# Products of the values-keys matrix with the output weight: three fp16 passes of split halves in place of one fp32 matmul each

## The chip, the cores and the metric

The kernel runs on one core of a Trainium2 chip. The metric is device time in microseconds of one execution; smaller is better.

## The reference, cut to what matters

```python
xn = _layernorm(x)                                     # x is [1250, 1024]
x = x + gnn(xn, edge_index, W, b) + mix(xn[None], Wq, bq, ..., Wo, bo)[0]
x = x + ffn(_layernorm(x)[None], clip_x, clip_down, w_gate, w_up, w_down)[0]

def mix(x, ...):                                       # H = 16 heads of DH = 64
    q = relu(split_heads(x @ Wq + bq))
    k = relu(split_heads(x @ Wk + bk))
    v = split_heads(x @ Wv + bv)
    context = einsum('bhld,bhkd->bhlk', q, k) / (l * DH)
    attn = einsum('bhlk,bhkd->bhld', context, v)
    return attn @ Wo + bo                              # heads side by side
def gnn(x, edge_index, W, b):                          # self loops, symmetric norm
    h = x @ W
    return relu(segment_sum(h[src] * norm[:, None], dst) + b)
```

There is no softmax between q k and v, so attn @ Wo = q @ M, where M is, for each head, (k^T v) / (l DH) times that head's rows of Wo. The kernel forms M once: it is [1024, 1024].

## The kernel before, in words

Nodes lie in T = 10 tiles of 128 rows (1250, the last is short). Matmuls of x with a weight are done in fp16: both sides are scaled by 256 and split into a high half and a low half (value minus high), and three products (high high, high low, low high) are added in PSUM. One such product of a 128-row tile with a 512-column half of a weight is 8 x 3 = 24 matmuls (node_unit, L498 to L516, the matmul is L509).

The order of work, written out by hand on each engine: keys and values in two column halves (with the counting of edges beside them), q, the graph projections g, the matrix M, then tile by tile (tile_b) the aggregation over edges (L687), q @ M (L713) and the residual, then the feed-forward part.

What the change touches lies between g and tile_b:

- **g tiles.** h over two column halves, t over ten tiles. TensorE (g_tile, L612) writes tile t into proj[t % 2] and waits before it for S["h_lo"] of tile t - 2, whose bank it takes. ScalarE (L870 to L877) writes the high half h16 from PSUM, signal h_hi; VectorE (L1205 to L1213) the low half, signal h_lo. Both have a hardware loop over pairs of tiles, with the tile's address from a register. TensorE has a loop too, but tiles (0,0) and (0,1) stand ahead of it, with the degree sums (L623) between them.
- **kvs**, the keys-values products kv_acc (128x128 blocks for pairs of heads, the diagonal 64x64 blocks wanted). VectorE clears kvs (L1189, fp32, 128x1024) and copies four groups of diagonal blocks from PSUM with the scale (L1195). This stands in VectorE's queue behind the degrees and ahead of the first h_lo.
- **The products.** TensorE multiplies kvs (8 pairs of heads) with wo, 2 column halves of the output weight: 16 fp32 matmuls of 512 columns (L646), into four banks in turn (tp[0], tp[1], proj[0], proj[1]). Product 2 takes proj[0] and waits for all 20 h_lo. Product i >= 4 waits for m_lo of i - 4. ScalarE copies the high half into m16 (L883, signal m_hi), VectorE the low half (L1220, signal m_lo); after product 1's, VectorE also makes the counts of tile 0 in fp16 (a_tile, L1202).
- **SyncE** loads wo[0] once the degrees are summed and the column maxima are there (L336 to L338), wo[1] after g tile (0,9) (L339), into places that earlier weights have left. After product 7 come the gnn bias and x tiles 0 and 1 (L341 to L344), after product 15 the bias bo (L346) and the first feed-forward weights; these take the place of wo and of kvs.
- **After it.** VectorE's evacuation in tile_b (L1281, L1284) needs x with bo added by POOL (L457), which waits for bo (L453); TensorE's next aggregation into the same banks waits for VectorE.

The lines that a sentence can't say:

```python
m_bank = tp + proj
wo = [part(RAW, K, HALF), part(0, K, HALF)]
kvs = part(XT + T * D, PAIRS, P)                       # fp32
if i >= 4:                                             # L642, TensorE, product i
    pe.wait_ge(SM["m_lo"], i - 3)
elif i == 2:
    pe.wait_ge(S["h_lo"], 2 * T)
pe.matmul(m_bank[i % 4][:, :], kvs[:, p, :], wo[n][:, p, :], start=True,
          stop=True).then_inc(SM["prod_full"], 1)
step(dve.memset(kvs, 0.0))                             # L1189, VectorE
```

Of the kernel before, what the change touches and what calls it, by code (L numbers as in the profile page):

```python
# [53 lines left out]
def gps_layer(nc, x, src, dst, gnn_W, gnn_b, Wq, bq, Wk, bk, Wv, bv, Wo, bo,  # L54
              clip_x, clip_down, w_gate, w_up, w_down, out):
    with ExitStack() as ctx:
# [3 lines left out]
        def sems(*names):  # L60
            return {n: ctx.enter_context(nc.semaphore(n)) for n in names}
# [10 lines left out]
        def part(at, *dims, dt=F32):  # L72
            size = 1
            for d in dims:
                size *= d
            words = size * {F16: 2, BF16: 2, I8: 1}.get(dt, 4) // 4
            a = mem[:, at:at + words]
            if dt != F32:
                a = a.bitcast(dt)
            if len(dims) == 2:  # L80
                a = a.rearrange("p (a b) -> p a b", b=dims[1])
            if len(dims) == 3:
                a = a.rearrange("p (a b c) -> p a b c", b=dims[1], c=dims[2])
            return a
# [17 lines left out]
        xT = part(XT, 2 * K, NP, dt=F16)  # L102
        kvs = part(XT + T * D, PAIRS, P)
        assert XT + T * D + D == 8 * SLOT + 11 * D
# [3 lines left out]

        wo = [part(RAW, K, HALF), part(0, K, HALF)]
        m16 = [part(XT + i * SLOT, K, D, dt=F16) for i in range(2)]  # L110

# [56 lines left out]
        def col(n=1):  # L168
# [21 lines left out]
        SE = sems("e_hot", "e_mm")  # L190
        SM = sems("wo_in0", "wo_in1", "gb_in", "bo_in", "kvs", "sources", "deg_full", "deg_ready", "dinv", "prod_full",
                  "m_hi", "m_lo", "max_col", "max_T")
# [84 lines left out]
        def _(sp):  # L277
# [64 lines left out]
            sp.dma_start(gb_b, gnn_b.rearrange("(a n) -> a n", a=1).broadcast_to([P, D])).then_inc(SM["gb_in"], 16)  # L342
            sp.dma_start(x_t[0], x[0:P, :]).then_inc(SB["xb_in0"], 16)
            sp.dma_start(x_t[1], x[P:2 * P, :]).then_inc(SB["xb_in1"], 16)  # L344
            sp.wait_ge(SM["prod_full"], 2 * PAIRS)
# [127 lines left out]
        def _(pe):  # L473
# [164 lines left out]
            for n in range(2):  # L638
                pe.wait_ge(SM[f"wo_in{n}"], 16)
                for p in range(PAIRS):  # L640
                    i = PAIRS * n + p
                    if i >= 4:  # L642
                        pe.wait_ge(SM["m_lo"], i - 3)
                    elif i == 2:
                        pe.wait_ge(S["h_lo"], 2 * T)
                    pe.matmul(m_bank[i % 4][:, :], kvs[:, p, :], wo[n][:, p, :], start=True,  # L646
                              stop=True).then_inc(SM["prod_full"], 1)

# [127 lines left out]
        def _(act):  # L776
# [91 lines left out]


            for h in range(2):  # L870
                with act.Fori(0, T // 2) as t2:
                    for par in range(2):
                        t = 2 * t2 + par
                        act.wait_ge(S["g_full"], T * h + t + 1)
                        act.wait_ge(SM["dinv"], 3)
                        act.activation(h16[:, bass.ds(t, 1), h * HALF:(h + 1) * HALF].rearrange("p a n -> p (a n)"),  # L876
                                       proj[par][:, :], ACT.Copy, scale=dinv_up[:, bass.ds(t, 1)]).then_inc(S["h_hi"], 1)  # L877


            for i in range(2 * PAIRS):  # L880
                n, p = i // PAIRS, i % PAIRS
                act.wait_ge(SM["prod_full"], i + 1)
                act.activation(m16[0][:, p, n * HALF:(n + 1) * HALF], m_bank[i % 4][:, :], ACT.Copy).then_inc(SM["m_hi"], 1)  # L883

# [73 lines left out]
        def _(dve):  # L958
# [232 lines left out]
            for b in range(2):  # L1191
                acc = kv_acc[b][:, :].rearrange("p (q n) -> p q n", n=P)
                for h in range(2):
                    r = slice(h * DH, (h + 1) * DH)
                    dve.tensor_scalar(kvs[r, 4 * b:4 * b + 4, r], acc[r, :, r], M_UP / (N * DH), None,  # L1195
                                      ALU.mult).then_inc(SM["kvs"], 1)

# [5 lines left out]


            for h in range(2):  # L1205
                with dve.Fori(0, T // 2) as t2:
                    for par in range(2):
                        t = 2 * t2 + par
                        dve.wait_ge(S["h_hi"], T * h + t + 1)
                        high, low = [h16[:, bass.ds(t, 1), a * D + h * HALF:a * D + (h + 1) * HALF].rearrange("p a n -> p (a n)")  # L1210
                                     for a in range(2)]
                        dve.scalar_tensor_tensor(low, proj[par][:, :], dinv_up[:, bass.ds(t, 1)], high, ALU.mult,  # L1212
                                                 ALU.subtract).then_inc(S["h_lo"], 1)  # L1213


            for i in range(2 * PAIRS):
                n, p = i // PAIRS, i % PAIRS
                dve.wait_ge(SM["m_hi"], i + 1)
                s = slice(n * HALF, (n + 1) * HALF)
                dve.tensor_tensor(m16[1][:, p, s], m_bank[i % 4][:, :], m16[0][:, p, s], ALU.subtract).then_inc(SM["m_lo"], 1)  # L1220
                if i == 1:
                    a_tile(0, 0)
# [188 lines left out]
```

## Time and profile before

| | |
|---|---|
| median of 3 runs | 761.18 us (760.9 to 761.96) |
| the profiled execution's own time | 761.22 us |
| its span, first to last instruction | 759.4 us |
| mean granted TensorE clock over the span | 0.981 of full |
| TensorE matmuls busy | 720.4 us, 95% |
| VectorE, ScalarE, GpSimd (POOL) busy | 490.1, 216.3, 272.1 us |
| L509 matmuls (all uses of node_unit) | 1440, 327.6 us busy, mean 381 ns |
| L646 as traced | 32 records for the 16 products |

How to read it: times are microseconds from the start of the span, unless marked ns. PE is TensorE's matmuls, PEld its weight loads, which run beside them; DVE is VectorE, ACT ScalarE, POOL GpSimd, SP SyncE. Matmuls are pipelined: a record (380 ns for 512 columns) is longer than the time from one start to the next, so the pace is read from a stretch with its count. A trailing bracket is idle time of the engine ahead of the row, and what ended it. ACTq and DVEq are the sequencers of these engines, with register work and waits. The chain of waits is followed back from the last instruction: at each step to what released it, or to the instruction before it on its engine.

### The profile page before, as it was taken

The page shows a single profiled execution, that of the slowest core. Times are in us where ns is not written, and L with a number is a line of the kernel's source. Part 1 is how long each engine was busy: PE and PEld are TensorE (multiplying, and loading weights), DVE is VectorE, ACT ScalarE, POOL GpSimd, SP SyncE. Part 2 cuts the span into 40 slices and gives each one's busy share as a digit, 9 for nine tenths or more (in the row PEclk, how much of TensorE's full clock was granted, in tenths as well). Part 3 has the DMA queues.
Part 4 walks back from the last instruction along what each step waited for, and adds up shares of the span by engine and source line. Part 5 has one row for each costly group of instructions (what it writes and reads, how often), then busy time and mean ns, then how long its engine had stood idle before and what let it go on. Part 6 is the DMA issues. An engine that isn't in the chain of part 4 may idle for free.

```text
span 759.4 us, 12399 instructions
## 1 busy us (share of the span) xinstructions
PE 720.4 (95%) x3889; PEld 370.9 (49%) x3892; DVE 490.1 (65%) x968; ACT 216.3 (28%) x363; POOL 272.1 (36%) x403
## 2 busy tenths in 40 slices
PE   4999999999999999999999999999999999994984
PEld 2455555555555544666544444444444444443551
DVE  7878887887666565557711111677777797757467
ACT  5133235542333244454111111401101110013450
POOL 5567677997666565530100000111111101110018
PEclk9999999999999999999999999999999999997997
DMA  9743322640000000003200300501111120000006
GB/s 344 215 123 71 91 55 73 197 164 13 0 0 0 0 2 1 2 1 111 84 28 0 110 0 0 163 26 56 57 49 48 48 66 30 22 0 1 1 13 258
DMA packets 35166, 47.87 MB, mean 63 GB/s; under 512 B 18883, under 2 KB 19915, under 8 KB 35121
## 3 DMA queue, kind: packets, MB, share of 16 engines
q1 hardware_dynamic: 35120, 47.28, 19.6%
q8 instruction: 27, 0.44, 0.2%
q14 instruction: 19, 0.15, 0.1%
HBM read 37.96 MB, written 5.12 MB: 57 GB/s over the span
## 4 chain that ended last, share of the span: by engine, by line
PE 73%; issue 13%; DVE 6%; POOL 4%; ACT 1%; DMA 1%; DVEq 1%; POOLq 0%; SPq 0%; ACTq 0%
PE bank L509 31%; PE bank L582 14%; PE bank L713 12%; PE bank L687 10%; POOL mem L468 2%; PE bank L494 2%; PE bank L646 2%; DVE mem L1001 2%; PE bank L526 2%; DVE counts L1091 1%; ACT mem L796 1%; DMA mem<-in_x 1%; DVE mem L1017 1%; POOL cols L396 1%; DVE hot_dst L1078 0%
## 5 line engine op out<-in xcount | busy, mean ns | idle before, releaser
L509 PE MATMUL bank<-mem 128*128 128x512 f16 x1440 | 327.6, 381 | 3.3 <-ACT mem L796 2.0
L509 PEld LDWEIGHTS bank<-mem 128*128 (+1 forms) x1440 | 137.9, 98 | 156.5 <-issue 5.1
L420 POOL TENSOR_SCALAR hot_src<-iota_p,src_col 125x128 bf16<-125x128 bf16 x252 | 174.5, 707 | 14.1 <-issue 14.1
L1091 DVE TENSOR_TENSOR counts<-bank,counts 128x120 f32 x328 | 92.4, 282 | 49.2 <-issue 8.4
L582 PE MATMUL bank<-mem 128*128 128x384 f16 (+1 forms) x576 | 107.5, 344 | 0.0
L713 PE MATMUL bank<-mem 128*128 128x512 f16 x480 | 105.4, 379 | 0.0
L687 PE MATMUL bank<-mem 128*128 128x512 f16 x400 | 88.0, 379 | 0.0
L582 PEld LDWEIGHTS bank<-mem 128*128 128x128 f16 (+1 forms) x576 | 55.3, 98 | 43.6
L713 PEld LDWEIGHTS bank<-mem 128*128 128x128 f16 x480 | 46.7, 98 | 54.3
L1212 DVE SCALAR_TENSOR_TENSOR mem<-bank,cols,mem 128x512 f32 x20 | 15.0, 751 | 81.8 <-ACT mem L876 81.8
L816 ACT ACTIVATE src_gap<-iota_p,loT 125x128 bf16<-125x128 bf16 x84 | 33.6, 399 | 115.2 <-PE bank L494 106.6
L459 POOL TENSOR_TENSOR cols<-cols 128x1 f32<-128x1 f32 x10 | 5.6, 555 | 166.5 <-DVE cols L1301 166.5
L457 POOL TENSOR_TENSOR mem<-mem 128x1024 f32<-128x1024 f32 x10 | 23.5, 2346 | 114.5 <-DMA mem<-in_L_mix_bo 114.5
L687 PEld LDWEIGHTS bank<-mem 128*128 128x128 f16 x400 | 39.1, 98 | 47.3 <-issue 0.6
L1078 DVE TENSOR_TENSOR hot_dst<-iota_w,keyT 125x480 bf16<-125x480 bf16 x84 | 55.1, 658 | 0.0
L417 POOL COPY src_col<-loT 125x3 f32 (+1 forms) x84 | 25.7, 306 | 69.6 <-PE bank L494 64.8
L1001 DVE SCALAR_TENSOR_TENSOR mem<-mem 128x2048 f16<-128x2048 f32 x16 | 36.8, 2303 | 6.7 <-ACT mem L796 6.7
L876 ACT ACTIVATE mem<-bank,cols 128x512 f32 x20 | 13.7, 687 | 91.9 <-PE bank L509 82.5
L1291 DVE SCALAR_TENSOR_TENSOR mem<-bank,mem 128x512 f32<-128x512 f32 x20 | 13.8, 692 | 40.0 <-PE bank L713 39.9
L468 POOL TENSOR_TENSOR mem<-mem 128x720 f32<-128x720 f32 (+1 forms) x10 | 18.7, 1897 | 50.6 <-DVE mem L1385 50.6
L494 PEld LDWEIGHTS bank<-hot_dst,hot_src 125*128 125x128 bf16 x328 | 24.5, 97 | 20.7 <-DVE counts L1091 1.9
L796 ACT ACTIVATE mem<-mem 128x2048 f16<-128x2048 f32 x16 | 30.4, 1904 | 14.7 <-DMA mem<-in_L_mix_Wk 6.0
(153 smaller groups left out, 681.8 us busy)
## 6 DMA issues: line engine op xcount, KB each, us to landing
mem<-in_x SPq DMA_DIRECT2D x18, 512.0 KB, 3.6
out_x<-mem SPq DMA_DIRECT2D x9, 512.0 KB
mem<-in_L_mix_Wk SPq DMA_DIRECT2D x4, 1024.0 KB, 9.4
mem<-in_L_mix_Wv SPq DMA_DIRECT2D x4, 1024.0 KB, 8.4
mem<-in_L_mix_Wq SPq DMA_DIRECT2D x4, 1024.0 KB, 5.2
mem<-in_L_gnn_W SPq DMA_DIRECT2D x4, 1024.0 KB, 5.2
mem<-in_L_mix_Wo SPq DMA_DIRECT2D x2, 2048.0 KB, 7.9
mem<-in_L_ffn_w_down SPq DMA_DIRECT2D x4, 352.0 KB, 3.0
```

The costliest lines, as they stand in the source:

```text
L420: pool.tensor_scalar(hot_src[0:EC, i, c, :], iota_p[0:EC, :], src_col[0:EC, i, c:c + 1], None, ALU.is_equal).then_inc(S["hot_src_ready"], 1)
L468: pool.tensor_tensor(x2[:, t, s], x2[:, t, s], y_t[t % 4][:, s], ALU.add).then_inc(SC["y_ready1"], 1)
L494: last = pe.matmul(agg[i][:, c * WC:(c + 1) * WC], hot_src[0:EC, i, c, :], hot_dst[0:EC, i, c, :], start=(c == 0), stop=True, skip_group_c ...
L509: last = pe.matmul(o[:, :], xT[:, a * K + k, bass.ds(t * P, P)], w16[i][:, k, b, :], start=(at == 0), stop=(at == len(parts) - 1))
L582: last = pe.matmul(proj[j % 2][:, 0:n * P], w_q.rearrange("p a n -> p (a n)"), xT[:, a * K + k, t0 * P:(t0 + n) * P], start=(k == 0 and a ...
L687: last = pe.matmul(agg[n][:, :], a_t[par][:, s, :], h16[:, s, b * D + n * HALF:b * D + (n + 1) * HALF], start=(fresh and s == 0 and b == 0 ...
L713: last = pe.matmul(proj[n][:, :], q_k, m16[b][:, k, n * HALF:(n + 1) * HALF], start=(k == 0 and a == b), stop=(k == K - 1 and a == 1))
L796: act.activation(w16[i][:, 4 * c:4 * c + 4, 0, :], w_raw[i][:, 4 * c:4 * c + 4, :], ACT.Copy, scale=W_UP).then_inc(S["w_hi"], 1)
L816: act.activation(src_gap[0:EC, i, :], iota_p[0:EC, :], ACT.Abs, bias=loT[0:EC, bass.ds(g * G + G - 1, 1)], scale=-1.0).then_inc(S["src_gap ...
L1001: dve.scalar_tensor_tensor(w16[i][:, s, 1, :], w_raw[i][:, s, :], W_UP, w16[i][:, s, 0, :], ALU.mult, ALU.subtract).then_inc(S["w_lo"], 1)
L1078: dve.tensor_tensor(hot_dst[0:EC, i], iota_w[0:EC], key, ALU.is_equal).then_inc(S["hot_dst_ready"], 1)
L1091: dve.tensor_tensor(window, agg[i][:, k * WC:(k + 1) * WC], window, ALU.add).then_inc(S["adj_added"], 1)
```

## The change

The products run as three fp16 matmuls of 512 columns each. For this, kvs becomes fp16 with a high and a low half (the same bytes), and the output weight is split into halves, 256 times as large, beside the g tiles: ScalarE's and VectorE's loops over the g tiles are written out, and after tiles (0,4), (0,7), (1,4) and (1,6) each takes a quarter of the weight (128x2048). The halves lie partly where earlier quarters of wo were. The evacuations of the products scale by 1/256; VectorE's turns from a subtraction into a multiply-subtract. SyncE's load of x tile 1 waits for four more products, since its place now holds halves of the weight.

```diff
--- before.py
+++ after.py
@@ -100,13 +100,15 @@
         bq_rows = part(QT + 6 * D, P)[0:K]
         XT = QT + T * D
         xT = part(XT, 2 * K, NP, dt=F16)
-        kvs = part(XT + T * D, PAIRS, P)
+        kvs = part(XT + T * D, 2 * PAIRS, P, dt=F16)
         assert XT + T * D + D == 8 * SLOT + 11 * D
         sources = part(RAW, NP)
         w16_q = part(2 * SLOT, 4 * K, HALF, dt=F16)
         h16 = part(2 * SLOT, T, 2 * D, dt=F16)
 
         wo = [part(RAW, K, HALF), part(0, K, HALF)]
+        wo16 = [[part(at, K, HALF, dt=F16) for at in ats] for ats in ((EXTRA, RAW), (RAW + 2 * D, 0))]
+        WO_AFTER = {(0, 4): (0, 0), (0, 7): (0, 1), (1, 4): (1, 0), (1, 6): (1, 1)}
         m16 = [part(XT + i * SLOT, K, D, dt=F16) for i in range(2)]
 
         x2 = part(QT - D, T, D)
@@ -188,7 +190,7 @@
                  "k_relu", "kv_done", "q_full", "x_hi", "x_lo", "xT_in0", "xT_in1", "src_gap", "hot_src_act", "counts_diag", "q_relu", "q_hi", "q_lo", "g_full", "h_hi", "h_lo", "hot_dst_ready",
                  "hot_src_ready", "adj_mm", "adj_added", "counts_set")
         SE = sems("e_hot", "e_mm")
-        SM = sems("wo_in0", "wo_in1", "gb_in", "bo_in", "kvs", "sources", "deg_full", "deg_ready", "dinv", "prod_full",
+        SM = sems("wo_in0", "wo_in1", "gb_in", "bo_in", "kvs", "kvs_hi", "wo_hi", "wo_lo", "sources", "deg_full", "deg_ready", "dinv", "prod_full",
                   "m_hi", "m_lo", "max_col", "max_T")
         SB = sems("xb_in0", "xb_in1", "x_bias", "a_ready", "mix_full", "agg_full", "mix_moved", "agg_moved",
                   "b_var", "b_rstd", "b_max", "a_more", "a_more_used")
@@ -341,6 +343,7 @@
             sp.wait_ge(SM["prod_full"], PAIRS)
             sp.dma_start(gb_b, gnn_b.rearrange("(a n) -> a n", a=1).broadcast_to([P, D])).then_inc(SM["gb_in"], 16)
             sp.dma_start(x_t[0], x[0:P, :]).then_inc(SB["xb_in0"], 16)
+            sp.wait_ge(SM["prod_full"], PAIRS + 4)
             sp.dma_start(x_t[1], x[P:2 * P, :]).then_inc(SB["xb_in1"], 16)
             sp.wait_ge(SM["prod_full"], 2 * PAIRS)
             sp.dma_start(bo_b, bo.rearrange("(a n) -> a n", a=1).broadcast_to([P, D])).then_inc(SM["bo_in"], 16)
@@ -636,15 +639,19 @@
 
             pe.wait_ge(SM["kvs"], 4)
             for n in range(2):
-                pe.wait_ge(SM[f"wo_in{n}"], 16)
                 for p in range(PAIRS):
                     i = PAIRS * n + p
+                    if p in (0, 4):
+                        pe.wait_ge(SM["wo_hi"], 2 * n + p // 4 + 1)
+                        pe.wait_ge(SM["wo_lo"], 2 * n + p // 4 + 1)
                     if i >= 4:
                         pe.wait_ge(SM["m_lo"], i - 3)
                     elif i == 2:
                         pe.wait_ge(S["h_lo"], 2 * T)
-                    pe.matmul(m_bank[i % 4][:, :], kvs[:, p, :], wo[n][:, p, :], start=True,
-                              stop=True).then_inc(SM["prod_full"], 1)
+                    for a, b in ((0, 0), (0, 1), (1, 0)):
+                        last = pe.matmul(m_bank[i % 4][:, :], kvs[:, a * PAIRS + p, :], wo16[n][p // 4][:, 2 * (p % 4) + b, :],
+                                         start=(a == b), stop=(a == 1))
+                    last.then_inc(SM["prod_full"], 1)
 
 
             def piece(i):
@@ -867,20 +874,27 @@
             act.activation(clip[:, 2:4], clip[:, 0:2], ACT.Exp, scale=-1.0).then_inc(SC["exp"], 1)
 
 
+            def wo_high(n, c):
+                act.wait_ge(SM[f"wo_in{n}"], 16)
+                act.wait_ge(SM["wo_lo"], 2 * n + c)
+                act.activation(wo16[n][c].rearrange("p (k b) n -> p k b n", b=2)[:, :, 0, :], wo[n][:, 4 * c:4 * c + 4, :], ACT.Copy,
+                               scale=W_UP).then_inc(SM["wo_hi"], 1)
+
             for h in range(2):
-                with act.Fori(0, T // 2) as t2:
-                    for par in range(2):
-                        t = 2 * t2 + par
-                        act.wait_ge(S["g_full"], T * h + t + 1)
-                        act.wait_ge(SM["dinv"], 3)
-                        act.activation(h16[:, bass.ds(t, 1), h * HALF:(h + 1) * HALF].rearrange("p a n -> p (a n)"),
-                                       proj[par][:, :], ACT.Copy, scale=dinv_up[:, bass.ds(t, 1)]).then_inc(S["h_hi"], 1)
+                for t in range(T):
+                    act.wait_ge(S["g_full"], T * h + t + 1)
+                    act.wait_ge(SM["dinv"], 3)
+                    act.activation(h16[:, t, h * HALF:(h + 1) * HALF], proj[t % 2][:, :], ACT.Copy,
+                                   scale=dinv_up[:, t:t + 1]).then_inc(S["h_hi"], 1)
+                    if (h, t) in WO_AFTER:
+                        wo_high(*WO_AFTER[h, t])
 
 
             for i in range(2 * PAIRS):
                 n, p = i // PAIRS, i % PAIRS
                 act.wait_ge(SM["prod_full"], i + 1)
-                act.activation(m16[0][:, p, n * HALF:(n + 1) * HALF], m_bank[i % 4][:, :], ACT.Copy).then_inc(SM["m_hi"], 1)
+                act.activation(m16[0][:, p, n * HALF:(n + 1) * HALF], m_bank[i % 4][:, :], ACT.Copy,
+                               scale=1.0 / W_UP).then_inc(SM["m_hi"], 1)
 
 
             act.wait_ge(SC["c_step"], 1)
@@ -1193,7 +1207,14 @@
                 for h in range(2):
                     r = slice(h * DH, (h + 1) * DH)
                     dve.tensor_scalar(kvs[r, 4 * b:4 * b + 4, r], acc[r, :, r], M_UP / (N * DH), None,
-                                      ALU.mult).then_inc(SM["kvs"], 1)
+                                      ALU.mult).then_inc(SM["kvs_hi"], 1)
+            for b in range(2):
+                acc = kv_acc[b][:, :].rearrange("p (q n) -> p q n", n=P)
+                for h in range(2):
+                    r = slice(h * DH, (h + 1) * DH)
+                    dve.wait_ge(SM["kvs_hi"], 2 * b + h + 1)
+                    dve.scalar_tensor_tensor(kvs[r, PAIRS + 4 * b:PAIRS + 4 * b + 4, r], acc[r, :, r], M_UP / (N * DH),
+                                             kvs[r, 4 * b:4 * b + 4, r], ALU.mult, ALU.subtract).then_inc(SM["kvs"], 1)
 
             def counts_tile(t):
                 return counts[:, bass.ds(t * P * T, P * T)].rearrange("p (n s) -> p s n", s=T)
@@ -1202,22 +1223,28 @@
                 dve.tensor_scalar(a_t[par], counts_tile(t), float(COUNT_MAX), None, ALU.min).then_inc(SB["a_ready"], 1)
 
 
+            def wo_low(n, c):
+                dve.wait_ge(SM["wo_hi"], 2 * n + c + 1)
+                high, low = [wo16[n][c].rearrange("p (k b) n -> p k b n", b=2)[:, :, a, :] for a in range(2)]
+                dve.scalar_tensor_tensor(low, wo[n][:, 4 * c:4 * c + 4, :], W_UP, high, ALU.mult,
+                                         ALU.subtract).then_inc(SM["wo_lo"], 1)
+
             for h in range(2):
-                with dve.Fori(0, T // 2) as t2:
-                    for par in range(2):
-                        t = 2 * t2 + par
-                        dve.wait_ge(S["h_hi"], T * h + t + 1)
-                        high, low = [h16[:, bass.ds(t, 1), a * D + h * HALF:a * D + (h + 1) * HALF].rearrange("p a n -> p (a n)")
-                                     for a in range(2)]
-                        dve.scalar_tensor_tensor(low, proj[par][:, :], dinv_up[:, bass.ds(t, 1)], high, ALU.mult,
-                                                 ALU.subtract).then_inc(S["h_lo"], 1)
+                for t in range(T):
+                    dve.wait_ge(S["h_hi"], T * h + t + 1)
+                    high, low = [h16[:, t, a * D + h * HALF:a * D + (h + 1) * HALF] for a in range(2)]
+                    dve.scalar_tensor_tensor(low, proj[t % 2][:, :], dinv_up[:, t:t + 1], high, ALU.mult,
+                                             ALU.subtract).then_inc(S["h_lo"], 1)
+                    if (h, t) in WO_AFTER:
+                        wo_low(*WO_AFTER[h, t])
 
 
             for i in range(2 * PAIRS):
                 n, p = i // PAIRS, i % PAIRS
                 dve.wait_ge(SM["m_hi"], i + 1)
                 s = slice(n * HALF, (n + 1) * HALF)
-                dve.tensor_tensor(m16[1][:, p, s], m_bank[i % 4][:, :], m16[0][:, p, s], ALU.subtract).then_inc(SM["m_lo"], 1)
+                dve.scalar_tensor_tensor(m16[1][:, p, s], m_bank[i % 4][:, :], 1.0 / W_UP, m16[0][:, p, s], ALU.mult,
+                                         ALU.subtract).then_inc(SM["m_lo"], 1)
                 if i == 1:
                     a_tile(0, 0)
             dve.wait_ge(SM["prod_full"], 2 * PAIRS)
```

## Rows read from the trace of the kernel before

**Rows 1.** The page, busy time of the engines.

```profile
PE 720.4 (95%) x3889; PEld 370.9 (49%) x3892; DVE 490.1 (65%) x968; ACT 216.3 (28%) x363; POOL 272.1 (36%) x403
```

**Rows 2.** Chain of waits, 360 to 510: start us, us, what (count).

```profile
374.04 98.47 PE bank L509 x456
...
472.73 0.70 ACT mem L876
...
473.72 0.76 DVE mem L1212
...
474.52 12.28 PE bank L646 x28
486.81 8.63 PE bank L687 x40
...
505.80 4.32 PE bank L687 x20
```

**Rows 3.** Timeline of the products: start us, us, engine, line, operation, shapes, count.

```profile
472.34 1.88 PE L646 MATMUL bank<-mem 128*128 128x512 f32 x4
...
474.38 1.28 DVE L1220 TENSOR_TENSOR mem<-bank,mem 128x512 f16<-128x512 f32 x2
...
475.58 1.31 DVE L1202 TENSOR_SCALAR mem<-counts 128x1280 f16<-128x1280 uint16 x1
...
476.80 1.92 DVE L1220 TENSOR_TENSOR mem<-bank,mem 128x512 f16<-128x512 f32 x3
...
478.26 0.60 ACT L883 ACTIVATE mem<-bank 128x512 f16<-128x512 f32 x1 [0.26 <-PE bank L646]
...
478.89 0.69 DVE L1220 TENSOR_TENSOR mem<-bank,mem 128x512 f16<-128x512 f32 x1 [0.17 <-ACT mem L883]
...
479.75 0.69 DVE L1220 TENSOR_TENSOR mem<-bank,mem 128x512 f16<-128x512 f32 x1 [0.17 <-ACT mem L883]
```

**Rows 4.** Groups by form: busy us, mean ns | idle us before, releaser.

```profile
L1001 DVE SCALAR_TENSOR_TENSOR mem<-mem 128x2048 f16<-128x2048 f32 x16 | 36.8, 2303 | 6.7 <-ACT mem L796 6.7
...
L1284 DVE SCALAR_TENSOR_TENSOR mem<-bank,mem 128x512 f32<-128x512 f32 x20 | 13.8, 692 | 1.5
...
L1023 DVE MEMSET cols<- 128x256 f32 x1 | 0.3, 272 | 0.1
...
L796 ACT ACTIVATE mem<-mem 128x2048 f16<-128x2048 f32 x16 | 30.4, 1904 | 14.7 <-DMA mem<-in_L_mix_Wk 6.0 <-DMA mem<-in_L_mix_Wv 3.6 <-DMA mem<-in_L_mix_Wq 2.8
```

**Rows 5.** Timeline 371 to 381, columns as in rows 3.

```profile
374.91 0.91 DVE L1189 MEMSET mem<- 128x1024 f32 x1 [0.28 <-DVE clip L1187]
375.86 1.78 DVE L1195 TENSOR_SCALAR mem<-bank 64x256 f32<-64x256 f32 x4
...
377.19 0.69 ACT L876 ACTIVATE mem<-bank,cols 128x512 f32 x1 [9.37 <-POOL cols L451]
378.18 0.75 DVE L1212 SCALAR_TENSOR_TENSOR mem<-bank,cols,mem 128x512 f32 x1 [0.54 <-ACT mem L876]
379.08 1.84 PEld L509 LDWEIGHTS bank<-mem 128*128 x10 [0.36 <-issue]
```

**Rows 6.** The page, DMA issues: count, KB each, us to landing.

```profile
mem<-in_L_mix_Wo SPq DMA_DIRECT2D x2, 2048.0 KB, 7.9
```

**Rows 7.** Timeline after the products, columns as in rows 3.

```profile
491.40 2.35 POOL L457 TENSOR_TENSOR mem<-mem 128x1024 f32<-128x1024 f32 x1 [114.52 <-DMA mem<-in_L_mix_bo]
```

**Rows 8.** Timeline of TensorE alone, two idle times elsewhere, columns as in rows 3.

```profile
32.06 5.35 PE L509 MATMUL bank<-mem 128*128 128x512 f16 x24 [1.24 <-DVE mem L1017]
...
702.52 0.62 PE L736 MATMUL bank<-ident,mem 128*128 128x128 bf16 x8 [2.17 <-DVE mem L1341]
```

**Rows 9.** Windows: busy PE, PEld, DVE, ACT, POOL, then granted clock, DMA share, GB/s.

```profile
32.00:34.00 2.00, 1.94 (x9) 0.90 (x10) 1.48 (x3) 1.01 (x2) 0.00 (x0) 1.00 0.08 17
...
704.00:706.00 2.00, 1.85 (x9) 1.67 (x9) 0.11 (x1) 1.78 (x3) 0.00 (x0) 0.50 0.00 0
706.00:708.00 2.00, 1.93 (x7) 0.84 (x7) 1.93 (x4) 0.00 (x0) 0.00 (x0) 0.71 0.00 0
```

## The prediction

> **What bounds the kernel now.** I read the page first: TensorE is busy 95% of the span [rows 1], so only what TensorE issues, or what makes it wait, can move the end. The chain of waits around the changed place says where. It runs through TensorE alone for 456 matmuls of the graph projections (L509, tiles (0,1) to (1,9), 98.47 us), which is 0.2159 us per fp16 matmul of 512 columns; leaves it for one evacuation on ScalarE and one on VectorE; then takes 12.29 us of L646 (from 474.52 to 486.81) and enters the aggregation L687 [rows 2]. Everything from L687 on is one serial stretch of TensorE, so a microsecond gained or lost before 486.81 reaches the end, unless a later load is missed.
>
> The timeline of the products shows their neighbours. VectorE's low halves (L1220) start 0.86 us apart, 0.03 us after ScalarE's 0.60 us: they follow TensorE's fp32 pace of 0.86 us per product. When VectorE is behind it goes faster: three take 1.92 us, so with 0.69 us for each record the starts are 0.61 apart. After the first two stands the count conversion L1202, with 1.22 us from its start to the next L1220 [rows 3].
>
> **The products.** An fp32 product costs 0.86 us; three fp16 passes cost 3 x 0.2159 = 0.648. Their weight loads run beside them, as L509's do. For the 14 products behind the wait for the last h_lo this is 14 x 0.86 = 12.04 against 9.07: **-2.97 us**. (12.29 - 12.04 = 0.25 is the first weight load and the last drain; it stays.) The first two products gain nothing: they end at 472.34 + 1.30 = 473.64 and the third must still wait for h_lo.
>
> That wait gets shorter, since both evacuation loops are written out. Now ScalarE starts 0.22 us after TensorE's end (472.51 to 472.73) and VectorE 0.29 after ScalarE's end [rows 2]; the written-out L1220 starts 0.03 after its releaser [rows 3]. I take 0.03 for VectorE and 0.05 for ScalarE: **-0.42 us**, product 2 at 474.10 instead of 474.52. Bounds: 0 and -0.5. At the other 18 tile ends the shorter lags gain nothing, TensorE being a tile ahead.
>
> What is late next is VectorE. h_lo starts at 473.29, m_lo 0 follows 0.66 later as now (473.72 to 474.38), m_lo 1 at 474.55, the conversion at 475.15, m_lo 2 at 476.37 and ends at 477.06. Product 6 uses its bank again and could start at 474.20 + 4 x 0.648 = 476.79, but starts 0.14 (signal and weight load) after 477.06: **+0.41 us**. After that VectorE's 0.61 and ScalarE's 0.60 stay under 0.648, and TensorE sets the pace. L1220 becomes a multiply-subtract from PSUM; L1284, the same kind on 128x512, has 0.692 us [rows 4], as L1220 has. The pace of 0.61 is bounded above by 0.69 (a rival, below). ScalarE's constant scale costs nothing here.
>
> Products together: -2.97 - 0.42 + 0.41 = **-2.98 us**.
>
> **The key-value matrix.** It is made ahead of h_lo 0, and this isn't hidden. Now the memset starts at 374.91 and takes 0.91, L1195 starts at 375.86 and its four take 1.78 (to 377.64); VectorE then waits 0.54 for ScalarE, and h_lo 0 ends at 378.93. TensorE's weight load of tile (0,2), which wants bank 0 back, comes at 379.08 after 0.36 of idle [rows 5]. So h_lo 0 has no slack: each further VectorE microsecond stands on the path.
>
> Added are four multiply-subtracts of 64x256 from PSUM, the form of the tensor_scalars with one more input. Four of those are 1.78, or 0.45 from start to start; I take 4 x 0.45 = 1.81. None of the four overlapped the one before it, so it is no less than 4 x 0.42 = 1.7; from above 4 x 0.69 = 2.8, L1284's full-size record [rows 4], which is far off, having twice the columns. The own-engine wait on kvs_hi is four instructions old and met, save for the pipeline.
>
> The memset keeps its bytes but goes from 1024 fp32 to 2048 fp16 elements. No row has a 2-byte memset. By bytes it stays at 0.91. By elements: 256 take 0.272 [rows 4] and 1024 take 0.912, 0.833 ns each, so 2048 take 1.77, 0.85 more. Below, fewer than 0.91 would need packing that no row shows. I take 1.77, since size in elements is all that the rows show it to follow. The Trainium skill (VectorE: DVE Perf Modes, "Zero memsets can be issued as uint32 (trn2)") says a memset takes one cycle per element whatever the type, which speaks for the slow end; with its 0.96 GHz that would be 2.13 us for 2048, 1.2 more than now, but the same sum gives 1.07 for 1024 where the trace has 0.91, so its rate is not taken; the total by it would be 0.4 us higher.
>
> h_lo 0 then starts at 377.64 + 0.85 + 1.81 + 0.03 = 380.33 instead of 378.18: **+2.15 us**, all of it TensorE idle ahead of tile (0,2). ScalarE (h_hi 1) isn't behind it, and h_lo 1 is wanted only 5.2 us later.
>
> **The halves of the output weight.** Four splits of 128x2048: 1.90 us on ScalarE and 2.30 on VectorE each, by L796 and L1001, the same shapes [rows 4]. Behind h_hi and h_lo of a tile they end 0.05 + 0.70 + 1.90 + 2.30 + 0.1 = 5.1 us after its end, about when the next tile's ends (24 x 0.2159 = 5.18); h_lo there is due one tile after that. Cost nothing; if the load of Wo were missing they would block ScalarE, but it is issued at about 374, takes 7.9 us to land [rows 6], and the first split comes after tile (0,4), near 395; the second load is issued after tile (0,9) near 421 and used after tile (1,4).
>
> **Loads on SyncE.** x_t[1] now waits for product 12, and bo_b stands behind it. bo_b lands at 491.40 now, 4.6 us after L687's start; POOL adds 2.35 to 493.75, and VectorE's four evacuations (about 3 us) free the banks by 497, wanted at 505.80 [rows 2, 7]. Sharing the engines with x_t[1], of the same size, it is late by 4.6 at most: 8.8 us of slack. Weight pieces move along with product 16. Nothing.
>
> **Sum:** -2.98 + 2.15 = -0.83. The profiled execution took 761.22 (span 759.4), 0.04 over the median of 761.18: **760.4 us**. A measurement of this kernel can tell about 0.2%, 1.5 us, from no change, and the forecast lies inside that.
>
> **Rivals.** (1) The memset goes by bytes: the stall is 1.30, the net -1.68, 759.5 us. For it: the region is the same. Against: the element slope.
>
> (2) **The clock falls**: the new idle of TensorE at 379 is some 2.1 us. After an idle of 1.24 us at 32.06 the granted clock was 1.00; after one of 2.17 us at 702.52 it was 0.50 in 704 to 706 and 0.71 in 706 to 708 [rows 8, 9], the lower level, 1.2 GHz. [...] Against it: before 702 TensorE did short products with pauses, before 379 it streams 512 columns without one. Price: 2 x 0.50 + 2 x 0.29 = 1.58 us of streaming, net +0.75: slower than before, 762.0 us.
>
> (3) VectorE paces the products: each m_lo takes its full 0.69. m_lo 11 ends at 476.37 + 10 x 0.69 = 483.27, and L687 starts 0.38 later: net -0.45, 760.8 us. The Trainium skill (VectorE: DVE Perf Modes, "The DRAIN you can't avoid") has the next operation wait until the pipe is empty, which gives this case. The three in 1.92 us speak against it.
>
> **How the numbers follow.** Forecast 0.43, (1) 0.22, (2) 0.20, (3) 0.11, others 0.04. The range runs from (1) with the lags at their best, 759.1, to (2) with the multiply-subtracts 0.5 dearer, 762.5. Faster by over 0.2% needs -1.52: about half of (1), the tail of the forecast and part of the others, 0.26. Slower by over 0.2% needs (2) and more on top, 0.08. Same 0.66.
>
> **What would show it.** In the timeline: memset near 1.77; four multiply-subtracts near 0.42; h_lo 0 ending near 381.1; an idle of 2.1 at tile (0,2), granted clock 1.00 behind it. h_lo 19 starting 0.8 after TensorE's end, not 1.2. Products 0.65 apart from product 7 on, one short stall before product 6. The stretch from the end of L509 to L687 14.3 - 3.0 = 11.3 us. L713 and the tiles after as before. I am wrong if h_lo 0 has slack, if the clock is below 1 behind 381, or if products wait for m_lo throughout.

## The result, and the profile after

| | before | changed |
|---|---|---|
| median | 761.57 us (760.9 to 762.85, 6 runs) | 759.25 us (758.75 to 759.92, 6 runs) |
| ratio | | 0.9968, 95% interval 0.9955 to 0.9981 |
| profiled execution, own time (span) | 761.22 (759.4) | 759.92 (758.1) |

The change makes the kernel 0.3% faster, 2.4 us by the ratio (1.4 to 3.4 by its interval). The forecast was 760.4 in a range of 759.1 to 762.5, with "same within 0.2%" as the likeliest outcome (0.66); the ratio lies outside those 0.2%, the end of its interval touches them. The time is near that of rival (1), 759.5, but rival (1) saves 1.68 us and 2.4 were measured.

In the page of the changed kernel TensorE is as full as before:

```profile
PE 719.2 (95%) x3908; PEld 370.0 (49%) x3908; DVE 500.2 (66%) x976; ACT 223.7 (30%) x367; POOL 272.1 (36%) x403
```

The chain of waits from 360 to 520, which answers to [rows 2] (start us, us, what, count):

```profile
366.36 5.18 PE bank L512 x24
...
373.80 100.12 PE bank L512 x456
473.92 0.02 issue
473.94 0.70 ACT mem L887
474.64 0.02 issue
474.66 0.75 DVE mem L1236
475.41 1.20 DVE mem L1246 x2
476.61 1.25 DVE mem L1223
477.86 0.61 DVE mem L1246
...
478.51 6.65 PE bank L652 x30
485.16 8.63 PE bank L694 x40
```

Read it in two pieces. From the end of the g tiles to L694 (the aggregation, L687 before) it takes 485.16 - 473.92 = 11.24 us, where before it took 486.81 - 472.51 = 14.30: -3.06. Inside it the chain leaves TensorE for VectorE's two low halves, the conversion L1223 and the third low half, as the prediction's step had it. But the 456 matmuls of the g tiles take 100.12 us, against 98.47 in [rows 2]: 1.65 more. That wasn't expected. The timeline from 371 to 392 answers to [rows 5]:

```profile
374.67 0.91 DVE L1203 MEMSET mem<- 128x1024 uint32 x1 [0.28 <-DVE clip L1201]
...
375.61 1.78 DVE L1209 TENSOR_SCALAR mem<-bank 64x256 f16<-64x256 f32 x4
...
377.42 1.78 DVE L1216 SCALAR_TENSOR_TENSOR mem<-bank,mem 64x256 f16<-64x256 f32 x4
...
379.24 0.75 DVE L1236 SCALAR_TENSOR_TENSOR mem<-bank,cols,mem 128x512 f16<-128x512 f32 x1
380.70 0.69 ACT L887 ACTIVATE mem<-bank,cols 128x512 f16<-128x512 f32 x1 [3.28 <-PE bank L512]
```

The memset is one of 1024 uint32 elements and takes 0.91 us, not 1.77. The four multiply-subtracts take 1.78, as forecast. h_lo 0 ends at 379.99, 1.3 us later than 378.93 when both are counted from the degrees (373.70 here, 373.95 before). And yet TensorE shows no idle: tile (0,1) itself ends only near 380.6 (ScalarE's h_hi 1, which follows it, starts at 380.70). The windows of 2 us say why (busy PE, PEld, DVE, ACT, POOL, then the granted clock):

```profile
374.00:376.00 2.00, 2.00 (x9) 0.75 (x7) 1.65 (x5) 0.00 (x0) 1.95 (x1) 0.67 0.49 112
376.00:378.00 2.00, 2.00 (x6) 0.76 (x5) 1.84 (x6) 0.69 (x1) 0.51 (x2) 0.50 1.03 382
378.00:380.00 2.00, 2.00 (x10) 0.88 (x9) 1.90 (x4) 0.00 (x0) 0.00 (x0) 0.97 1.05 410
```

The granted clock is at its lower level (0.50, 1.2 GHz) for most of tile (0,1), right behind the degree sums. Tile (0,1) becomes longer than VectorE's delay and covers it. Before, all windows from 372 to 380 had 1.00 in the profiled execution; the middle one:

```profile
376.00:378.00 2.00, 2.00 (x11) 0.90 (x10) 1.55 (x4) 0.69 (x1) 0.70 (x3) 1.00 1.00 376
```

One pair of profiles, then, can't price the four multiply-subtracts, and it had to be asked whether the fall of the clock belongs to the change.

### The profile page after: what moved, and what is told of

The parts are those of the page before. It is cut to its first block, busy times and chain, and to the rows that moved or that the text cites. A ratio compares the mean times of both kernels' runs of the same rounds, so it can differ in the third digit from the quotient of the medians.

```text
span 758.1 us, 12288 instructions
## 1 busy us (share of the span) xinstructions
PE 719.2 (95%) x3908; PEld 370.0 (49%) x3908; DVE 500.2 (66%) x976; ACT 223.7 (30%) x367; POOL 272.1 (36%) x403
## 4 chain that ended last, share of the span: by engine, by line
PE 73%; issue 13%; DVE 7%; POOL 4%; ACT 1%; DMA 1%; DVEq 1%; POOLq 0%; SPq 0%
PE bank L512 31%; PE bank L585 14%; PE bank L720 12%; PE bank L694 10%; POOL mem L471 2%; PE bank L497 2%; DVE mem L1015 2%; PE bank L529 2%; DVE counts L1105 1%; ACT mem L803 1%; PE bank L652 1%; DMA mem<-in_x 1%; DVE mem L1031 1%; POOL cols L399 1%; DVE hot_dst L1092 0%
## 5 line engine op out<-in xcount | busy, mean ns | idle before, releaser
L694 PE MATMUL bank<-mem 128*128 128x512 f16 x400 | 88.0, 379 | 0.0
L694 PEld LDWEIGHTS bank<-mem 128*128 128x128 f16 x400 | 39.1, 98 | 47.0
L1236 DVE SCALAR_TENSOR_TENSOR mem<-bank,cols,mem 128x512 f16<-128x512 f32 x20 | 15.0, 751 | 67.8 <-ACT mem L887 67.8
L887 ACT ACTIVATE mem<-bank,cols 128x512 f16<-128x512 f32 x20 | 13.8, 688 | 86.1 <-PE bank L512 76.9
L826 ACT ACTIVATE hot_src<-src_gap,cols 125x128 bf16<-125x128 bf16 x84 | 33.7, 402 | 2.7
```

Source lines behind the costliest of these rows:

```text
L694: last = pe.matmul(agg[n][:, :], a_t[par][:, s, :], h16[:, s, b * D + n * HALF:b * D + (n + 1) * HALF], start=(fresh and s == 0 and b == 0 ...
L826: act.activation(hot_src[0:EC, i, G - 1, :], src_gap[0:EC, i, :], ACT.Relu, bias=ones[0:EC], scale=-1.0).then_inc(S["hot_src_act"], 1)
```

## The experiments

Two theories. **A**: the products save about 3.05 us; the work ahead of h_lo 0 costs about 1.3 us of TensorE idle, except in executions in which the clock falls in tile (0,1). **B**: the work ahead of h_lo 0 never stands on the path. To keep them from the noise of the rest of the kernel (the g tiles start anywhere from 366.36 to 367.42 in these profiles), I take from each profile the stretch from the start of g tile (0,0) to the start of the aggregation, both read in the chain of waits. In the kernel before, the stretch begins with this line (its end, 486.81, is in [rows 2]):

```profile
366.61 5.18 PE bank L509 x24
```

The fourth column is the same question for an earlier place, 14 to 18 us, long before anything that the change touches.

| kernel | stretch, us | clock fell at 374 to 378 | at 14 to 18 | median, us (runs) | ratio to before, 95% interval |
|---|---|---|---|---|---|
| before | 486.81 - 366.61 = 120.20 | no | yes | 761.57 (6) | |
| changed | 485.16 - 366.36 = 118.80 | yes | no | 759.25 (6) | 0.9968 [0.9955, 0.9981] |
| after_again | 485.67 - 366.86 = 118.81 | yes | no | 759.21 (8) | 0.9966 [0.9951, 0.998] |
| kvs_later | 485.95 - 367.16 = 118.79 | yes | no | 759.22 (10) | 0.9967 [0.9954, 0.9979] |
| loops_out | 486.59 - 366.88 = 119.71 | no | yes | 761.13 (12) | 0.9993 [0.9981, 1.0005] |
| four_more | 488.73 - 366.88 = 121.85 | yes | no | 762.57 (12) | 1.0008 [0.9997, 1.0019] |
| degrees_before | 486.44 - 366.85 = 119.59 | no | no | 760.62 (12) | 0.9986 [0.9975, 0.9996] |
| degrees_after | 484.24 - 366.37 = 117.87 | no | no | 757.75 (5) | 0.9954 [0.994, 0.9967] |
| degrees_kvs_later | 483.95 - 367.42 = 116.53 | no | no | 757.59 (5) | 0.9952 [0.9939, 0.9966] |
| memset_elements | 488.14 - 366.75 = 121.39 | no (later) | yes | 760.42 (10) | 0.9987 [0.9977, 0.9998] |
| waits_only | 485.10 - 366.63 = 118.47 | no | yes | 759.0 (1) | |
| a_tile_later | 485.27 - 366.84 = 118.43 | yes | no | 759.58 (1) | |
| products_both | 484.26 - 366.61 = 117.65 | no | yes | 758.29 (1) | |
| all_four | 482.40 - 366.72 = 115.68 | no | no | 756.9 (6) | 0.9938 [0.9923, 0.9953] |

The three kernels with one execution each serve for their stretch alone. Outside the stretch the fourteen profiled executions took between 639.9 and 641.9 us, so whole times differ by up to 2 us for reasons that lie elsewhere.

The two columns on the clock belong together. Of the ten profiles with all the degree sums in a row, the five that fell at 14 to 18 us did not fall at 374 to 378, and the five that did not fall there all fell at 374 to 378; each group holds kernels with the old and with the new products. The fall at 14 to 18 is in this line of the kernel before (0.56; the changed kernel has 1.00 there):

```profile
14.00:16.00 2.00, 1.89 (x6) 0.59 (x5) 2.00 (x3) 1.77 (x1) 2.00 (x3) 0.56 1.06 393
```

So whether the clock falls in tile (0,1) differs from execution to execution and goes with something that is there long before the changed place. Why the two exclude each other no run shows.

### The changed kernel again

No edit.

> The changed kernel once more, beside the parts below. Theory A (the chain of TensorE: the products save 3.06 us, the four multiply-subtracts ahead of h_lo 0 cost 1.3 us of TensorE idle, unless the granted clock falls behind the degree sums and makes tile (0,1) about 1.7 us longer, which hides them): times in two clusters, 1.7 to 1.8 us under the clean executions of before without that fall, 3.06 under those with it. Theory B (the multiply-subtracts never stand on the path): 3 us under before in both. Median 759.3 in A, 758.2 in B.

Median 759.21 (758.56 to 760.48), beside 29 runs of before with a median of 761.19 (760.39 to 763.79). The stretch is 118.81, the clock fell again. The lowest runs are 1.83 apart (758.56 and 760.39), the highest 3.31. That leans to A, but no more: the lowest and highest of 8 runs are set beside those of 29, and no pair of clusters is to be seen. Both kernels spread evenly, the rest of the kernel adding its own differences.

### kvs later

```diff
-            step(dve.memset(kvs, 0.0))
-            ...
+            def make_kvs():
+                step(dve.memset(kvs, 0.0))
+                ...
             for h in range(2):
                 for t in range(T):
                     ...
+                    if (h, t) == (0, 1):
+                        make_kvs()
```

> The whole making of kvs is moved behind h_lo of tile (0,1), so nothing but the degrees stands ahead of h_lo 0. Theory A: 1.3 us less than the changed kernel where the clock does not fall in tile (0,1), the same where it does; the idle at tile (0,2) is gone. 3.0 us under before in every execution. Theory B: as the changed kernel.

The profile fell on an execution with the lower clock. Its chain of waits has the same g tiles:

```profile
374.59 100.12 PE bank L512 x456
```

The same 100.12 us with h_lo 0 ending at 379.09, more than 2 us before TensorE was through with tile (0,1) (h_hi 1, which follows it, ends just ahead of h_lo 1's start at 382.22): the extra 1.65 us is the clock alone, and nothing of VectorE's lateness stands behind it. The lowest run, 758.0, is 0.56 under after_again's and the medians are equal. The expected "3.0 under before in every execution" is not seen in the medians (2.0), so this run by itself leaves A and B open.

### The loops written out alone

```diff
-                with act.Fori(0, T // 2) as t2:
-                    for par in range(2):
+                for t in range(T):
...
-                with dve.Fori(0, T // 2) as t2:
-                    for par in range(2):
+                for t in range(T):
```

> The kernel before with ScalarE's and VectorE's loops over the g tiles written out, nothing else. My step says -0.42 us, between the end of L509 and the third product: ScalarE starts 0.05 after TensorE's end and VectorE 0.03 after ScalarE's. Rival: the register work was not on the path, 0.

The chain of waits doesn't leave TensorE any more:

```profile
374.32 98.42 PE bank L509 x456
472.74 13.85 PE bank L646 x32
```

13.85 us instead of 14.30: -0.45, where I had -0.42. In the time it can't be told (0.9993, the interval holds 1).

### Four more operations in the kernel before

```diff
+            for b in range(2):
+                ...
+                    dve.wait_ge(SM["kvs"], 2 * b + h + 1)
+                    dve.scalar_tensor_tensor(kvs[r, 4 * b:4 * b + 4, r], acc[r, :, r], M_UP / (N * DH),
+                                             kvs[r, 4 * b:4 * b + 4, r], ALU.mult, ALU.max).then_inc(SM["kvs"], 1)
...
-            pe.wait_ge(SM["kvs"], 4)
+            pe.wait_ge(SM["kvs"], 8)
```

> The kernel before with four more operations of 64x256 from PSUM ahead of h_lo 0 (a scaled copy again, kept as the maximum with itself: same values). h_lo 0 ends 1.8 - 0 us later than before's 378.93. Theory A: +1.7 us where the clock does not fall in tile (0,1), the idle standing ahead of tile (0,2); 0 to 0.3 where it falls. Theory B: 0 always.

```profile
374.32 100.12 PE bank L509 x456
```

The clock fell in this profile, so the fall is no property of the new products. The stretch is 121.85 = 120.20 + 1.65: with the fall, four operations ahead of h_lo 0 cost nothing. That they cost without it this run doesn't show, as its one profile has the fall. The times lean that way (the median of 12 runs is 1.38 above before's, the lowest 1.29 above the lowest of 29), but the ratio of 1.0008 makes it 0.6 us, with an interval that holds no change.

### The degree sums inside tile (0,0)

The 20 one-column matmuls (10 sums, two passes each) stand between g tiles (0,0) and (0,1) for 2.1 us. Seven sums can be taken earlier:

```diff
+                    if at % 3 == 2 and at // 3 < len(degrees):
+                        degree(degrees[at // 3])
...
-            g_tile(0, 0, 0)
-            pe.wait_ge(SM["sources"], 1)
-            for n in range(T):
+            g_tile(0, 0, 0, degrees=range(7))
+            for n in range(7, T):
```

For this VectorE signals each quarter of the counts as it is done (src_part, not shown), and each sum waits for its own quarter.

> The changed kernel, with seven of the ten degree sums issued between the matmuls of g tile (0,0) and only three behind it. The stretch of one-column matmuls, after which the granted clock fell to 0.5 in three of four profiles, shrinks from 2.1 to about 0.7 us, and its weight loads run beside the 512-column matmuls. Theory A: no fall at 374 to 378, one cluster of times instead of two; the stretch itself saves 1.4 us; h_lo 0 has no cover, so TensorE idles 1.3 us at tile (0,2). About 757.4 us. If the fall has another cause it stays in most executions, tile (0,1) takes 1.7 us more and the times lie in two clusters again.

> The same, with kvs made behind h_lo of tile (0,1). Theory A: 1.3 us under degrees_after in every execution, about 756.1, and no idle at tile (0,2). Theory B (the multiply-subtracts never on the path): equal to degrees_after.

> The kernel before with seven degree sums inside g tile (0,0). No fall of the clock at 374 to 378, about 1.5 us under before, 759.6, in one cluster. The difference to degrees_after is then what the change is worth without the clock's part: -3.06 + 1.2 = -1.9 us.

In degrees_after the cost stands bare. The timeline:

```profile
378.65 1.41 DVE L1239 SCALAR_TENSOR_TENSOR mem<-bank,cols,mem 128x512 f16<-128x512 f32 x2
...
379.56 8.80 PE L512 MATMUL bank<-mem 128*128 128x512 f16 x40 [1.18 <-DVE mem L1239]
```

h_lo 0 ends at 379.41, TensorE starts 0.15 later, after 1.18 us of idle. (In the chain the stall is a little longer than that idle: from the start of g tile (0,0) to the end of the g tiles before has 472.51 - 366.61 = 105.90, and waits_only, which has the same idle of 1.18, 473.85 - 366.63 = 107.22, so 1.32 more.) The chain of waits now runs through the memset, the four copies, the four multiply-subtracts and h_lo 0. With kvs made later it does not. The g tiles in its chain:

```profile
374.25 98.44 PE bank L512 x456
...
483.95 8.63 PE bank L699 x40
```

against, in degrees_after,

```profile
379.56 93.43 PE bank L512 x432
...
484.24 8.63 PE bank L699 x40
```

The stretch is 116.53 against 117.87: 1.34 us for the order of VectorE's work alone. **Within the stretch this shows A's mechanism.** The time does not show it: 756.1 was expected and 757.59 measured, beside 757.75 for degrees_after, five runs each. What hides it is at least in part the clock elsewhere. The five runs of degrees_after have a mean granted clock of 0.9838 over the span, those of degrees_kvs_later 0.9818, and in the 61 runs of before beside these experiments the 19 at 0.983 or more have a median of 760.9, the 42 below it 761.95. In the profile of degrees_kvs_later, for one, TensorE idles 2.40 us at 31.82 and has a clock of 0.50 behind it, which none of the others has. That the 1.34 us reach the end is thus argued, not shown.

And the change itself, without the fall on either side: 119.59 to 117.87, -1.72 us. (The runs say more, 760.62 to 757.75; by the ratios 0.9986 and 0.9954 it is 2.4 us, with about 1 us of uncertainty on each. They don't contradict 1.72 and don't confirm it.) The same comes from before and waits_only (below), whose products last as long as the changed kernel's: 120.20 to 118.47, -1.73. With the fall on both sides, taking four_more for what before would be there (the one profile of before has no such fall): 121.85 to 118.80, -3.05.

The saving of the move I had too large: 1.4 to 1.5 us expected, 120.20 - 119.59 = 0.61 found. A sum between 512-column matmuls still takes 0.12 us of TensorE in the chain, against 0.21 in the row of twenty. By the ratio the runs gained 1.1 us; the 0.5 beyond the stretch would fit a fall that no longer comes in part of the executions. The profiles speak for that: of those without a fall at 14 to 18, five of five fell at 374 to 378 with the sums in a row, and none of the four with seven of them moved. (The move also shifts all behind it by 0.6 us, and no run separates the two.) The times still spread as widely as before (759.33 to 762.22), and "one cluster" was wrong.

### The memset by elements

```diff
-            step(dve.memset(kvs, 0.0))
+            step(dve.memset(kvs[:, :, 0:1], 0.0))
+            step(dve.memset(kvs[:, :, 1:P], 0.0))
```

> The changed kernel with kvs cleared in two pieces (column 0 of each block, then the other 127), which can't be read as 4-byte words. My step said 0.833 ns per element whatever its size: the memset of 2032 fp16 elements takes 1.76 us instead of 0.91, h_lo 0 ends 0.95 later (with the 0.1 of the small piece). If it goes by bytes: 0.91. Time: up to 0.9 over the changed kernel where the clock does not fall, about 0.3 to 0.9 where it does.

```profile
375.46 1.75 DVE L1204 MEMSET mem<- 128x2032 f16 x1 [0.49 <-DVE mem L1203]
...
381.79 6.39 PE L512 MATMUL bank<-mem 128*128 128x512 f16 x21 [2.42 <-DVE mem L1237]
```

The element rate holds: 1.75 us for 2032 two-byte elements, 0.833 ns each by the slope from [rows 4]. TensorE idles 2.42 us, 1.24 more than the 1.18, where 0.95 was expected: 0.84 is the memset, and the small piece ahead of it costs 0.40 and not 0.1, since the second memset starts 0.49 behind its end. And behind that idle comes what rival (2) described. The windows:

```profile
382.00:384.00 2.00, 2.00 (x8) 0.78 (x7) 0.28 (x1) 0.00 (x0) 0.00 (x0) 0.75 0.00 0
384.00:386.00 2.00, 2.00 (x6) 0.73 (x5) 0.00 (x0) 0.00 (x0) 0.00 (x0) 0.50 0.00 0
386.00:388.00 2.00, 2.00 (x9) 0.83 (x8) 0.00 (x0) 0.00 (x0) 0.00 (x0) 0.90 0.03 8
```

The chain has, for tiles (0,2) to (1,9) of this kernel and then of waits_only:

```profile
381.79 95.11 PE bank L512 x432
```

```profile
380.43 93.42 PE bank L512 x432
```

The fall costs 1.69 us; I had priced it 1.58. The stretch adds up: 118.47 + 1.24 + 1.69 = 121.40, found 121.39. The ratio has it 1.3 to 1.5 us above the changed kernel, more than the 0.9 expected.

### Product 2's wait, and the conversion

```diff
-                    elif i == 2:
-                        pe.wait_ge(S["h_lo"], 2 * T)
+                    elif i >= 2:
+                        pe.wait_ge(S["h_lo"], 2 * T - 3 + i)
```

```diff
-                if i == 1:
+                if i == 11:
                     a_tile(0, 0)
```

waits_only has the first, a_tile_later the second, products_both both.

> The changed kernel, product 2 waiting for 19 of the 20 h_lo (its bank was tile (1,8)'s), product 3 for all. Product 2 starts 0.4 us earlier. But VectorE's third m_lo still comes after the conversion, and product 6 waits for it: the stretch from the end of L512 to L694 stays at 11.24 us within 0.1. Rival: TensorE sets the pace and the whole stretch is 0.4 shorter.

> Only the conversion moved. Product 2 still waits for the last h_lo, product 6 no longer for VectorE: the stretch from the end of L512 to L694 is 10.8 to 10.9 us, so that the 0.41 us that my sum had for VectorE's lateness is what the conversion cost.

> The changed kernel with product 2 waiting for 19 h_lo, and VectorE's conversion of the first counts moved from behind product 1's low half to behind product 11's. Nothing then holds a product: 16 x 0.648 us in one piece. From the end of L512 to L694 10.4 to 10.6 us instead of 11.24; L694 may wait 0.2 for the counts.

From the end of the g tiles to the aggregation: waits_only 485.10 - 473.85 = 11.25, a_tile_later 485.27 - 474.40 = 10.87, products_both 484.26 - 473.82 = 10.44, against 11.24. All three came as expected. In the last, L694 starts 0.05 behind the end of VectorE's conversion, so VectorE is then as near to setting the pace as TensorE. In the timeline of products_both the 48 matmuls are one piece:

```profile
473.65 10.52 PE L652 MATMUL bank<-mem 128*128 128x512 f16 x48
...
484.26 4.06 PE L694 MATMUL bank<-mem 128*128 128x512 f16 x18
```

An earlier start of product 2 is worth nothing while product 6 waits for VectorE, and 0.43 us once it doesn't.

### All of it

The four edits together on the changed kernel.

> The changed kernel with kvs made behind h_lo (0,1), the degree sums inside g tile (0,0), product 2's wait and the later conversion. From the start of the g tiles to L694 0.7 us less than degrees_kvs_later's 116.5; time about 756.8, 4.4 under before.

```profile
373.55 98.44 PE bank L512 x456
...
482.40 8.81 PE bank L699 x40
```

The stretch is 115.68, 0.85 less than degrees_kvs_later; median 756.9, ratio 0.9938: the version that beats both kernels.

## Why the prediction held in the range and missed the likeliest outcome

- **The fp16 products (-2.97), the loops (-0.42), VectorE's lateness (+0.41), together -2.98: right.** Measured -3.06 in the pair of profiles; the loops alone -0.45; the conversion moved away -0.37. Products run 6.65 us for ten, 0.665 each with the first load and the drain, and VectorE kept up: rival (3) falls. Twelve low halves took 7.70 us in products_both, 0.64 each, less than their 0.69. The Trainium skill (VectorE: DVE Perf Modes, "The DRAIN you can't avoid"), from which the rival had that an operation waits until the pipe is empty, adds in the same section that a next operation that is not held starts earlier; that is what these rows show.
- **The slack of h_lo 0 (none): right.** degrees_after has TensorE waiting for it, 0.15 us behind its end as in [rows 5]. The stall without the memset's term was to be 1.30 and is 1.32.
- **The splits of the output weight (nothing): right.** The 456 matmuls of the g tiles take 98.44 us beside them in degrees_kvs_later and 98.42 without them in loops_out.
- **Four multiply-subtracts (+1.81): right**, 1.78.
- **The memset (+0.85): wrong, and the step that cost the forecast.** I took the element count of the source, 2048; the instruction on the chip has 1024 uint32 elements and 0.91 us, so the term is 0. The rate I used was right (1.75 us for 2032 elements where no 4-byte form exists). The Trainium skill has it in the very section that the prediction cites for the slow end, "Zero memsets can be issued as uint32 (trn2)" (VectorE: DVE Perf Modes): zeros over 2-byte elements can go at 4 bytes per element, half the elements. The trace agrees, 1024 uint32. So the section speaks for rival (1), not against it. With 0 for this term my sum is -1.68, and the profiles without the fall give -1.72 and -1.73.
- **The clock: the mechanism was in rival (2), the place was missed.** Behind an idle of 1.18 us the clock stayed at 1.00, as behind 1.24 in [rows 8]; behind 2.42 it fell. The length of the idle does not settle it, though: in the kernel before it fell behind 1.97 us too (TensorE starts at 13.20, the line for 14 to 16 above), and in four_more it stayed at 1.00 behind 2.26 us at 704.66. What I did not see is that the 2.1 us of degree sums ahead of tile (0,1), busy though they are in the profile, can be followed by the same fall, in before too, and that it then hides VectorE's work. It fell in 5 of the 10 profiles with all the degree sums in a row. With a fall in half the executions the change would be worth between 1.73 and 3.05, about 2.4 us, which is what the ratio says (0.9968 of 761.6). How often it falls in runs without a profile was not measured, so that agreement is an estimate.
- **Loads: hidden, as costed.** POOL's first sum starts at 490.31, 5.2 us behind L694 where it was 4.6, and no later wait of TensorE names it.
- **That the time lies in the range is luck in part.** The range was built on 761.18 for the kernel before, which has 761.57 in the runs of the result; the ratio on 761.18 gives 758.7, below the lower end of 759.1. The sum as forecast, -0.83, was missed by 1.6 us, of which 0.85 is the memset and the rest, by the estimate above, the executions in which the fall hides the stall.

## What to carry to other kernels

Where the bound engine is one step from waiting, count every instruction ahead of its releaser, and put work that is wanted only much later (kvs was wanted 95 us on) behind it: 1.3 us of this stretch for moving lines. Cost an instruction by the form in which it is issued, not by the source's type. When a pair of profiles disagrees with the sum, compare one stretch over several profiles and look at the granted clock in it before naming a cause.

## What was not expected of the hardware

- TensorE's granted clock can fall to 0.50 behind a stretch in which it is busy, by the profile, but with one-column matmuls: 20 of them in 2.1 us, then 1.65 us lost in the next tile (100.12 against 98.47 us), in 5 of 10 profiles: exactly those in which it had not fallen at 14 to 18 us.
- The same engine kept its clock behind 1.18 us of idle and lost 1.69 us behind 2.42 us; between these it went either way (fallen behind 1.97 and 2.17 us, not behind 2.26).
- A zero memset of 2048 fp16 elements ran as 1024 uint32 in 0.91 us; cleared in rows of 127 elements it took 1.75 us for 2032.
- One-column fp32 sums between 512-column matmuls still took 0.12 us each in the chain, two passes together; they don't vanish beside them.
